# Two-layer graph network on one core: low halves written over their logits, adjacency rows loaded in quarters, last block reordered

## The reference, cut to what matters

```python
def reference(x, adj, L0_gnn_W, L0_gnn_a, L1_gnn_W, L1_gnn_b):   # x (2048, 256), adj (2048, 2048)
    h = relu(layernorm(x))
    ht = (h @ W0).reshape(N, 4, 256).transpose(1, 0, 2)            # 4 heads of 256
    src, dst = einsum('hnd,hd->hn', ht, a_src), einsum('hnd,hd->hn', ht, a_dst)
    e = leaky_relu(src[:, :, None] + dst[:, None, :], 0.01) + adj[None]
    x = x + einsum('hij,hjd->hid', softmax(e, -1), ht).mean(axis=0)
    h = relu(layernorm(x))
    A = (adj != 0)
    return x + A @ (h @ W1 + b1) / A.sum(axis=0)[:, None]
```

## Time and profile before

| | us |
|---|---|
| median of 3 runs | 620.12 (618.66 to 622.84) |
| profiled execution, its own time | 619.52 |
| its span | 617.4 |
| TensorE busy | 531.0 (86%) |
| VectorE busy | 457.0 (74%) |
| ScalarE busy | 462.6 (75%) |

### The profile page before, as it was taken

How to read it: one execution, slowest core, us unless ns; L and a number is a source line. 1 busy time by engine, 2 the same in 40 slices (tenths; PEclk the granted TensorE clock), 3 DMA queues, 4 the chain that set the end, 5 groups by cost and what they waited for, 6 DMA issues and landing times.

```text
span 617.4 us, 9010 instructions
## 1 busy us (share of the span) xinstructions
PE 531.0 (86%) x2991; PEld 303.0 (49%) x2991; DVE 457.0 (74%) x604; ACT 462.6 (75%) x391; POOL 30.8 (5%) x64
## 2 busy tenths in 40 slices
PE   6799569989898798989798898989798899777997
PEld 6333224545454454546454554544454455365885
DVE  5836665869678768878787888888778888263984
ACT  4647774979798878988898988888798886243861
POOL 4000000000000000000000000000000000000211
PEclk9879999989899989989999999999999999798999
DMA  8224151899999999999999999999999999941111
GB/s 321 62 102 184 35 102 35 153 225 179 227 225 206 217 188 213 206 213 206 221 223 209 226 203 230 200 221 193 219 230 206 227 198 201 233 131 58 43 42 42
DMA packets 300319, 108.91 MB, mean 176 GB/s; under 512 B 284748, under 2 KB 295372, under 8 KB 297724
## 3 DMA queue, kind: packets, MB, share of 16 engines
q1 hardware_dynamic: 300296, 108.62, 82.3%
HBM read 30.90 MB, written 6.39 MB: 60 GB/s over the span
## 4 chain that ended last, share of the span: by engine, by line
PE 27%; SPq 24%; ACT 15%; DMA 14%; issue 12%; DVE 7%; ACTq 0%; POOLq 0%; POOL 0%; DVEq 0%
SPq L296 12%; DMA probs_hi_t<-probs_hi 11%; PE ps_acc L736 11%; PE ps_relu L804 8%; SPq L304 7%; ACT logits L529 6%; ACT probs_hi L537 5%; SPq L314 3%; DVE logits L934 2%; ACT ps_relu L521 1%; PE ps_acc L714 1%; PE ps_h L714 1%; DMA x_all<-in_x 1%; DMA hidden_in<-hidden_scratch 1%; ACT x_all L452 1%
## 5 line engine op out<-in xcount | busy, mean ns | idle before, releaser
L736 PE MATMUL ps_acc<-h_w_split,probs_hi_t 128*128 128x512 f16 x1024 | 242.0, 391 | 48.7 <-DMA probs_hi_t<-probs_hi 47.3
L736 PEld LDWEIGHTS ps_acc<-h_w_split,probs_hi_t 128*128 128x128 f16 x1024 | 100.3, 100 | 171.2 <-DMA probs_hi_t<-probs_hi 54.2
L521 ACT ACTIVATE ps_relu<-dst_rows,src_bias 128x2048 f32<-128x2048 f32 x64 | 126.1, 1971 | 67.6 <-DVE small L934 67.4
L934 DVE CUSTOM_DVE_ANT_0 logits<-ps_relu,adj_rows 128x2048 f32<-128x2048 f32 x48 | 110.0, 2291 | 65.6 <-DMA adj_rows<-in_adj 33.8
L745 PE MATMUL ps_acc<-h_w_split,probs_lo_t 128*128 128x256 f16 x1024 | 122.7, 273 | 0.6 <-DMA probs_lo_t<-probs_lo 0.6
L943 DVE SCALAR_TENSOR_TENSOR probs_lo<-logits,small,probs_hi 128x2048 f16<-128x2048 f32 x48 | 112.7, 2349 | 0.3 <-ACT probs_hi L537 0.2
L745 PEld LDWEIGHTS ps_acc<-h_w_split,probs_lo_t 128*128 128x128 f16 x1024 | 96.3, 98 | 24.2 <-issue 10.4
L529 ACT ACTIVATE logits<-logits,small 128x2048 f32<-128x2048 f32 x48 | 95.4, 1988 | 0.0
L537 ACT ACTIVATE probs_hi<-logits,small 128x2048 f16<-128x2048 f32 x48 | 95.4, 1987 | 0.0
L804 PE MATMUL ps_relu<-hidden_split,mask_columns 128*128 128x512 f32 x256 | 62.9, 406 | 4.7 <-DVE hidden_split L1032 4.2
L804 PEld LDWEIGHTS ps_relu<-hidden_split,mask_columns 128*128 128x128 f32 x256 | 49.7, 195 | 16.6 <-DVE hidden_split L1032 4.8
(11 more groups left out here) (93 smaller groups left out, 380.4 us busy)
## 6 DMA issues: line engine op xcount, KB each, us to landing
adj_rows<-in_adj SPq DMA_DIRECT2D x16, 1024.0 KB, 6.1
dst_rows<-dst_scratch SPq DMA_DIRECT2D x3, 1024.0 KB, 6.3
x_all<-in_x SPq DMA_DIRECT2D x4, 512.0 KB, 6.1
x<-in_x SPq DMA_DIRECT2D x16, 128.0 KB, 2.5
x_scratch<-x SPq DMA_DIRECT2D x16, 128.0 KB, 1.9
hidden_scratch<-hidden SPq DMA_DIRECT2D x16, 128.0 KB, 2.2
out<-out_rows SPq DMA_DIRECT2D x16, 128.0 KB, 1.7
x_in<-x_scratch SPq DMA_DIRECT2D x1, 1792.0 KB, 8.1
```

Of the source, the lines that this page charges most:

```text
L521: nc.scalar.activation(R[:, :], D[:, h, :], ACT.Relu, scale=(1.0 - SLOPE) / SLOPE, bias=src[:, bass.ds(u, 1)]).then_inc(relu_ready, 1)
L736: last = nc.tensor.matmul(ACC[parity][:, :], TA[:, e, b, :], H[:, h, b, :], start=(h == 0 and b == 0), stop=False)
L934: nc.vector.tensor_tensor_reduce(out=logits_of(h, parity), in0=R[:, :], in1=ADJ[:, parity, :], scale=-1.0, scalar=3.0e38, op0=ALU.add, op1 ...
```

## The change

- There are four logits buffers E (128 x 4 x 2048 fp32). The logits of h=3 no longer lie in the adjacency rows.
- The low half is written in fp16 into the first half of its own logits row (low_rows); PB is gone. It no longer waits for an older transpose; instead logits(u) waits until the low transpose of unit u-4 has landed.
- The adjacency rows of block ib+2 are loaded in four column quarters of 512, one in each slot h of SP, ahead of that slot's low transpose. The first waits for the logits and the mask rows of block ib. VectorE waits for all four.
- mask_columns MC lies over the four logits buffers, h_t over the last two, deg and rdeg over src_bias.
- In the last block: on ScalarE the casts wait for low transposes only, and hidden_high(1) stands ahead of cast 0, h1_relu(14) after cast 1; on TensorE transpose_h1(14) stands ahead of the last low multiply, hidden(14) ahead of the first aggregate, hidden(15) after the first piece of 2 matmuls; on VectorE hidden_low and degree move one slot earlier, and x1_sum(15) and x1_stats(15) ahead of hidden(14); on SP load_hidden(1) stands in slot 1, and store_hidden(14) behind store_x1(15).

```diff
-        E = place("logits", [P, HEADS - 1, N], fp32)
         ADJ = place("adj_rows", [P, 2, N], fp32)
+        E = place("logits", [P, HEADS, N], fp32)
         PA = place("probs_hi", [P, 2, N], fp16)
-        PB = place("probs_lo", [P, 2, N], fp16)
...
-        HT = alias("h_t", [P, FK, N], fp32, "probs_hi")
+        HT = alias("h_t", [P, FK, N], fp32, "logits", 4 * 2 * N)
...
-        MC = alias("mask_columns", [P, BUFS, NB, P], f32r, "probs_hi")
+        MC = [alias(f"mask_columns{j}", [P, NB, P], f32r, "logits", 4 * j * N) for j in range(BUFS)]
...
-        def logits_of(h, parity):
+        def low_rows(h):
-            return E[:, h, :] if h < HEADS - 1 else ADJ[:, parity, :]
+            return E[:, h, :].bitcast(fp16)[:, 0:N]
...
-            def load_adj(ib, parity):
-                if isinstance(ib, int) and ib == 1:
-                    sp.wait_ge(pieces_ready, 1)
-                else:
-                    sp.wait_ge(probs_lo_ready, 4 * ib - 4)
+            def load_adj(ib, parity, h):
+                if h == 0:
+                    sp.wait_ge(logits_ready, 4 * ib - 4)
                     passed(ib)
-                sp.dma_start(ADJ[:, parity, :], adj[bass.ds(ib * P, P), :]).then_inc(adj_in[parity], 16)
+                    sp.wait_ge(mask_rows_ready, ib - 1)
+                    passed(ib)
+                c = slice(BANK * h, BANK * (h + 1))
+                sp.dma_start(ADJ[:, parity, c], adj[bass.ds(ib * P, P), c]).then_inc(adj_in[parity], 16)
...
+                if not (isinstance(ib, int) and ib + 2 >= NB):
+                    load_adj(ib + 2, parity, h)
                 if has(u + 2):
-                    transpose_lo(u + 2, h % 2)
-                if h == 2 and not (isinstance(ib, int) and ib + 2 >= NB):
-                    load_adj(ib + 2, parity)
+                    transpose_lo(u + 2, h % 2, (h + 2) % 4)
                 if h == 3 and not final(ib):
                     transpose_mask(ib + 1)
                 if final(ib) and h == 0:
-                    sp.wait_ge(probs_lo_ready, UNITS - 4)
+                    sp.wait_ge(logits_ready, UNITS - 4)
+                    load_hidden(0)
+                if final(ib) and h == 1:
+                    sp.wait_ge(logits_ready, UNITS)
                     sp.wait_ge(mask_in, 16 * NB)
-                    load_hidden(0)
-                if final(ib) and h == 2:
-                    sp.wait_ge(probs_lo_ready, UNITS)
                     load_hidden(1)
...
             load_hidden(2)
-            store_hidden(NB - 2)
             sp.wait_ge(unit_multiplied, UNITS - 3)
...
             store_x1(NB - 1)
+            store_hidden(NB - 2)
             store_hidden(NB - 1)
...
+                if final(ib) and h == 1:
+                    hidden_high(0)
                 if final(ib) and h == 2:
-                    hidden_high(0)
+                    hidden_high(1)
                     cast(0, 0, 0)
-                    hidden_high(1)
                 if final(ib) and h == 3:
                     cast(0, 1, 1)
+                    h1_relu(NB - 2)
...
-                elif q < 2:
-                    act.wait_ge(mask_in, 16 * NB)
-                    act.wait_ge(probs_lo_ready, UNITS)
-                    for e in range(2):
-                        act.wait_ge((hi_in, lo_in)[q][e], 16 * UNITS // 2)
                 else:
-                    act.wait_ge((hi_multiplied, unit_multiplied)[q - 2], UNITS)
+                    if q == 0:
+                        act.wait_ge(mask_in, 16 * NB)
+                    act.wait_ge(lo_in[q % 2], 16 * (UNITS // 2 - 1 + q // 2))
...
+                if final(ib) and h == 3:
+                    transpose_h1(ib - 1)
                 multiply_low(k, h, parity)
-                if h == 3 and past(ib, 1):
+                if h == 3 and past(ib, 1) and not final(ib):
                     transpose_h1(ib - 1)
...
+            hidden(NB - 2)
             pe.wait_ge(hid_lo_ready, 2)
             aggregate(0, 0, 0, split[1])
-            hidden(NB - 2)
             aggregate(1, 1, 0, split[1])
             transpose_h1(NB - 1)
             pe.wait_ge(hid_lo_ready, 3)
             aggregate(0, 0, split[1], split[2])
+            hidden(NB - 1)
             aggregate(1, 1, split[1], split[2])
             aggregate(2, 2, 0, split[2])
-            hidden(NB - 1)
...
             def logits(u, ib, h, parity):
                 if h == 0:
-                    vec.wait_ge(adj_in[parity], 8 * (ib - parity) + 16)
-                if h == 3:
-                    vec.wait_ge(mask_rows_ready, ib + 1)
-                if past(u, HEADS) and h < 3:
-                    vec.wait_ge(probs_lo_ready, u - HEADS + 1)
+                    adj_there(ib, parity)
+                if past(u, HEADS):
+                    vec.wait_ge(lo_in[h % 2], 8 * (u - h % 2) - 16)
...
-            def low(v, k, h, parity):
+            def low(v, h):
                 vec.wait_ge(probs_hi_ready, v + 1)
-                if past(v, 2):
-                    vec.wait_ge(lo_in[h % 2], 16 * k)
-                nc.vector.scalar_tensor_tensor(PB[:, h % 2, :], logits_of(h, parity), rinv[:, h:h + 1],
+                nc.vector.scalar_tensor_tensor(low_rows(h), E[:, h, :], rinv[:, h:h + 1],
                                                PA[:, h % 2, :], ALU.mult, ALU.subtract).then_inc(probs_lo_ready, 1)
...
-                if final(ib) and h == 2:
+                if final(ib) and h == 1:
                     hidden_low(0)
                     degree(0)
+                if final(ib) and h == 2:
                     hidden_low(1)
+                    degree(1)
                 if final(ib) and h == 3:
-                    degree(1)
                     degree(2)
...
+            x1_sum(NB - 1, 1)
+            x1_stats(NB - 1)
             hidden(NB - 2)
             hidden_low(2)
-            x1_sum(NB - 1, 1)
-            x1_stats(NB - 1)
```

More of the change, by code:

```diff
@@ L522, in relu_term, with exp @@
                                      bias=src[:, bass.ds(u, 1)]).then_inc(relu_ready, 1)
-            def exp(u, h, parity):
-                rows = logits_of(h, parity)
+            def exp(u, h):
+                rows = E[:, h, :]
                 act.wait_ge(logits_ready, u + 1)
@@ L530, in exp, with high @@
                                      bias=nmax[:, h:h + 1], accum_out=rsum[:, h:h + 1]).then_inc(probs_ready, 1)
-            def high(v, k, h, parity):
+            def high(v, k, h):
                 act.wait_ge(rinv_ready, v + 1)
@@ L543, in h1_relu, with slot @@
                                      ACT.Relu).then_inc(h1_ready, 1)
-            def slot(ib, h, parity):
+            def slot(ib, h):
                 u = 4 * ib + h
                 if has(u + 2):
-                    high(u + 2, 2 * ib + (h + 2) // 2, (h + 2) % 4, parity if h < 2 else 1 - parity)
+                    high(u + 2, 2 * ib + (h + 2) // 2, (h + 2) % 4)
                 if h == 0 and past(ib, 2):
@@ L578, in cast @@
                     last = nc.scalar.activation(
-                        MC[:, j, :, half * P // 2:(half + 1) * P // 2].rearrange("p (c s) m -> p c s m", s=2),
+                        MC[j][:, :, half * P // 2:(half + 1) * P // 2].rearrange("p (c s) m -> p c s m", s=2),
                         rows, ACT.Copy)
@@ L595, in _ @@
             hw_high(10)
-            exp(0, 0, 0)
+            exp(0, 0)
             for g in range(11, 14):
@@ L600, in _ @@
             hw_high(14)
-            exp(1, 1, 0)
-            high(0, 0, 0, 0)
+            exp(1, 1)
+            high(0, 0, 0)
             for g in range(15, 18):
@@ L606, in _ @@
             hw_high(18)
-            exp(2, 2, 0)
-            high(1, 0, 1, 0)
+            exp(2, 2)
+            high(1, 0, 1)
             for g in range(19, 22):
@@ L612, in _ @@
             hw_high(22)
-            exp(3, 3, 0)
+            exp(3, 3)
             for g in range(23, GROUPS):
@@ L618, in body @@
                 for h in range(HEADS):
-                    slot(ib, h, parity)
+                    slot(ib, h)
             block_loop(act, body)
-            h1_relu(NB - 2)
             cast(1, 0, 2)
@@ L803, in aggregate @@
                 for b in range(lo, hi):
-                    last = nc.tensor.matmul(AC[j], MC[:, j, b, :], HO[:, b, :],
+                    last = nc.tensor.matmul(AC[j], MC[j][:, b, :], HO[:, b, :],
                                             start=(b == 0), stop=(b == NB - 1))
@@ L999, in slot @@
                 if has(u + 2):
-                    low(u + 2, 2 * ib + (h + 2) // 2, (h + 2) % 4, parity if h < 2 else 1 - parity)
+                    low(u + 2, (h + 2) % 4)
                 if h == 0 and past(ib, 1):
@@ L1050, in _ @@
             hw_low(16)
-            low(0, 0, 0, 0)
+            low(0, 0)
             row_inverse(1, 1)
@@ L1056, in _ @@
             hw_low(20)
-            low(1, 0, 1, 0)
+            low(1, 1)
             row_inverse(2, 2)
```

30 lines of the change are left out of this document (16 added, 14 removed).

## The result

The changed kernel takes 648.69 us (646.87 to 651.99, 4 runs) against 619.59 us: ratio 1.0486, 95% interval 1.0429 to 1.0543. It is slower by 29 us, where 617.5 us was forecast with a range up to 627. The profiled execution has a span of 650.0 us. Ratios are estimated from the single executions, so they differ by up to 0.4% from the quotient of the medians. They leave out one of the four executions of pool_quarters, which ran in a slower state.

What follows compares the result with a forecast made beforehand. The prediction saw four resources close together and two closed chains of nearly equal length bounding the block. The loop's 0.0 and the last block's -2 us against 619.52 us gave 617.5 us, range 606 to 627.

Steps and rivals of the forecast that it cites:

- What bounds the kernel before: Repeating attention block: TensorE, ScalarE, VectorE and DMA stand close together; stalls are high transposes, 26.3 us, and adjacency rows, 22.7 us.
- TensorE's 2.00 and 0.88 us waits: Waits at the h=1 high transpose and the next multiply, laid to SP's congested transpose behind the 1 MB load; both go.
- The two chains named: Closed chains of nearly equal length in a block: through SP's congested transpose, and through the adjacency rows.
- Four logits rows, low halves in place: 0.: Logits buffers and low halves over their own logits: 0 taken, bounds 0 and +0.5 us a block for the new wait.
- The quarter loads: 0.0 us a block.: Four 256 KB loads in SP slots h=0 to 3: new block 27.24 us against 27.26, 0.0 us over 14 blocks.
- It lands at T + 6.0, and the logits start at T + 6.05: Fourth quarter's landing and next h=0 logits, counted from T, the h=1 high half's end on ScalarE; 5.52 before.
- SP has room: SP's queue: three more issues cost 1.1 to 1.7 us a block, the congested transpose gives back 2.7 us.
- relu of h=3 now starts when ScalarE is free: 5.9: ScalarE, step from relu of h=2 to relu of h=3: 5.9 us instead of 6.45, -0.55 a block.
- The walk: One block summed in five steps between successive h=0 logits: 6.89 + 2.51 + 5.90 + 5.89 + 6.05 = 27.24 us.
- The last block: -2 us.: New order of the last block: 3.6 - 5.4 - 1.0 = -2.8, taken as -2 us, bounds -4 and +2.
- The last quarter comes too late: Rival: fourth quarter queues behind transpose and x load, lands at T + 7.1, +1.0 us a block, 631 us; chance 0.15.
- The DMA engines are the bound: Rival: DMA share 1.06 is full, spreading bytes moves nothing, both waits stay, 620 us; chance 0.10.

Runs made afterwards that it cites:

- pool_quarters: Changed kernel with its four column quarters of a block issued by GpSimd as soon as the buffer is free, none by SP: 638.69 us, ratio 1.0292.
- one_slot0: Changed kernel with one 1 MB adjacency load in slot 0, ahead of the low transpose, instead of four quarters: 609.28 us, ratio 0.9822.
- early: Changed kernel with its four quarter loads issued in SP's slots 0, 0, 1, 2 instead of 0, 1, 2, 3: 630.14 us, ratio 1.0207.
- q4_first: Changed kernel with the fourth quarter issued in slot 3 ahead of the high transpose instead of behind it and the residual load: 640.73 us, ratio 1.0351.
- one_slot2: Changed kernel with one 1 MB load in slot 2 behind the low transpose, where the kernel before had it: 615.74 us, ratio 0.9945.
- warm: Changed kernel with 24 matmuls that add no result, into an unused half bank ahead of the h=1 seed: 648.26 us, ratio 1.0490.
- three_warm: Changed kernel with quarters 1 to 3 in slot 0, the fourth still in slot 3, and 24 idle matmuls ahead of the h=1 seed: 628.62 us, ratio 1.0133.
- slot0_old_end: one_slot0 with the old order of the last block on every engine: 612.00 us, ratio 0.9896.
- four_slot2: Changed kernel with its four column quarters issued together in slot 2, behind the low transpose: 626.05 us, ratio 1.0079.

## Why the prediction was wrong

**What bounds the kernel before** held in part. TensorE's 2.00 and 0.88 us waits did come from the transpose behind the 1 MB load: with the load elsewhere they fell from 26.3 to 3.5 us in the changed kernel and to 5.0 in one_slot0, whose block is as long as before. But that gained nothing in one_slot0's blocks, and early and q4_first have such waits (22.6 and 35.9 us) with small loads. The two chains named weren't all: SP itself waited only 3.8 us in nine blocks.

**Four logits rows, low halves in place: 0.** Held; one_slot2 shows it, with the last block's gain, at 615.74 us. The new wait was covered in the changed kernel as predicted, but it took 32.7 us in early and 19.6 in one_slot0, where the low transposes are late.

**The quarter loads: 0.0 us a block.** This failed; the block measures 30.31 us against my 27.24. By its terms (means of nine blocks):
- "It lands at T + 6.0, and the logits start at T + 6.05": they start at T + 8.11. Issue to logits was put at 2.90 us and is 3.94 (example: 339.59 to 343.67): +1.04. The fourth quarter's own landing, 3.2 to 3.6 us, was put at 2.85 from the 2.5 and 2.7 of the earlier trace rows, and some 0.4 us lie between a landing and the logits' start, which I had put at 0.05. The rows before show that gap too: 326.04 - 319.75 = 6.29 us against landings of 6.0. The issue itself comes at 8.11 - 3.94 = T + 4.17 instead of T + 3.15: SP is 0.89 us behind T instead of 0.16, the x load's issue takes 0.69 instead of 0.35 us.
- "SP has room", with nine transposes filling "only 20 of SP's 27.3 us". It hadn't. That count left out the four plain issues, 2.0 us, and the gaps between 13 instructions, and took the congested transpose at the median; all instructions take 23.25 us, and SP waited only 0.4 us a block. I added three more issues, took back 2.7 us for the one congested transpose, and let the low transposes take what they took. Those right behind a quarter, three in a block, take some 1.05 us more each, and the third quarter's issue takes 0.89 us (mean of eight). This is the step that failed in kind: SP runs from the h=2 low transpose to the fourth quarter, 319.65 to 339.59, nearly without a pause, then 3.94 us pass to the logits, and SP's stretch starts again when the low half behind them is ready (SP waits for it 9.5 us in eight blocks). The warm run shows this chain setting the block. What the next instruction of the queue pays was missing from the sum.
- "relu of h=3 now starts when ScalarE is free: 5.9": 6.88. The seed of h=1 did wait for the relu, 29.6 / 8 = 3.7 us instead of 1 to 2, TensorE's clock was down behind that wait, and the seed of h=2 was late. Given back, it gains only when SP's chain is cut (three_warm).

The walk's two terms that moved are 8.11 - 6.05 = 2.06 and 6.88 - 5.90 = 0.98, together 3.04 of the 3.07 us a block.

**The last block: -2 us.** Held. The timelines at the multiply of unit 60 and the aggregates behind the first, before and then after:

```profile
512.28 3.62 PE L736 MATMUL ps_acc<-h_w_split,probs_hi_t 128*128 128x512 f16 x16
...
568.37 2.92 PE L804 MATMUL ps_relu<-hidden_split,mask_columns 128*128 128x512 f32 x9 [0.49 <-ACT mask_columns L578]
```

```profile
547.05 3.62 PE L735 MATMUL ps_acc<-h_w_split,probs_hi_t 128*128 128x512 f16 x16
...
601.57 3.69 PE L805 MATMUL ps_relu<-hidden_split,mask_columns 128*128 128x512 f32 x15 [1.24 <-ACT mask_columns L578]
```

The last part took 568.37 - 512.28 = 56.1 us before and 601.57 - 547.05 = 54.5 after, 1.6 less; slot0_old_end gives 2.7 us by the medians. The loss lies ahead of it: 25.4 us from block 6 to 15, 2.83 a block, and 9.7 us from block 1 to 6, 1.9 a block (second table). The prediction's 14 equal blocks were too many for its per-block terms. The rows of the tail after, against the earlier trace rows:

```profile
589.72 0.38 PE L753 MATMUL ps_h<-ident,x_norm 128*128 128x128 f32 x2
...
590.57 1.13 PE L761 MATMUL ps_g<-w,h_t 128*128 128x256 f32 x4
...
591.35 8.98 PE L805 MATMUL ps_relu<-hidden_split,mask_columns 128*128 128x512 f32 x38
```

hidden(15) comes two matmuls after the transpose, and 38 matmuls follow without the 3.14 us wait.

**The rivals.** "The last quarter comes too late", given 0.15 and 631 us, was the right direction and place with under half the size (12 of 29 us). It took the fourth quarter's landing for the only price. Its sign came true: the adjacency wait went over 4 us a block. "The DMA engines are the bound" was wrong as put, since both waits did move and the time did not stay, but it isn't refuted for the kernels with one load in slots 0 to 2: their waits move and their nine blocks stay at 247.3 to 249.3 us.

The rule weighed in the prediction (the Trainium skill, DMA: Bandwidth & Descriptors, "Rules for kernel authors": coalesce many small transfers) was right: four_slot2 against one_slot2, 10.3 us for the same bytes in the same place, agrees with it. The other estimate, 2.0 us for a quarter, was further off than the rows' 2.7. The table it came from (the Trainium skill, DMA: Bandwidth & Descriptors, "Measured") counts the time in which the DMA engines are busy, for loads issued from GpSimd. The trace's time from issue to landing is 3.6 us.

## What to carry to other kernels

When a transfer is cut into pieces on a queue that also carries the critical transfers, price each piece by what it adds to the next instruction of the queue, not by its own issue and bytes; and before calling a queue free, add up all that it issues and look at its own waits. A buffer that comes free earlier can be used for a load that starts earlier: one_slot0 used the same buffers with the whole load in slot 0 and won 1.8% where the quarters lost 4.9%. But look where such a gain arises: here it was in the first and the last blocks, while in the repeating ones one wait had only been changed for another. And where two chains are within a microsecond, a test that shortens one of them can show nothing; look at which side waits for the other at the point where they meet.

## What was not expected of the hardware

- A DMA transpose issued right behind a 256 KB load takes SP 3.04 us instead of 1.98 (medians of the low transposes), one right behind a 1 MB load 4.9 to 5.2 us. Behind the 128 KB x load and x1 store of the kernel before the medians are 2.15 and 1.86 us, near the common one.
- Four loads cost more than one of their size: 10.3 us in columns and 17.8 us in partitions, in slot 2.
- Loads issued from GpSimd's queue aren't independent of SP's: the 128 KB x load landed in 7.0 us instead of 2.5 beside them.
- Behind 3.59 us of idle time TensorE ran a whole low multiply at the 1.2 GHz level (0.53 granted, 3.54 us instead of 1.92); with 24 matmuls in the gap the mean granted clock was 0.989.
